# Row-wise exponentials of 16 attention heads on ScalarE: one instruction over a shifted copy, or 16 instructions that read the scores with the row maximum as bias and give the row sum

## What is computed

```python
q = l2norm(q) * qs; k = l2norm(k) * ksc          # then rotary tables
sim = einsum('bhwie,bhwje->bhwij', bq, bk2) * QK_SCALE    # 32 x 64 scores, QK_SCALE = 8
sim = where(mask, -finfo.max, sim)
attn = softmax(sim, -1)                          # row maximum, exp, row sum
out = einsum('bhwij,bhwje->bhwie', attn, bv2)
x = (out @ Wo) + x
x = ffn_layer(shift_tokens(x)) + x
```

## Time and profile before

| | |
|---|---|
| time, median of 2 runs | 4887.01 us (4881.81 and 4892.21) |
| span of the profiled execution | 4869.5 us |
| what lies around the span | 12.3 us and 22.7 us against the two runs |
| busy: PE, DVE, ACT, POOL | 78%, 79%, 51%, 49% of the span |
| granted TensorE clock, mean | 0.905 |
| scalar exponentials of attention (L743) | 192, 1060 ns each |

### The profile page before, as it was taken

One profiled execution on the slowest core, in us unless ns is written; L12 is line 12 of the kernel. 1 busy time (PEld: TensorE's weight loads), 2 busy tenths in 40 slices (PEclk: granted clock), 3 DMA queues, 4 the chain that ended last, 5 costly groups with the idle time before them and its releaser, 6 DMA issues.

```text
span 4869.5 us, 152986 instructions
## 1 busy us (share of the span) xinstructions
PE 3785.1 (78%) x64080; PEld 2581.5 (53%) x64080; DVE 3828.5 (79%) x6082; ACT 2483.4 (51%) x3705; POOL 2389.1 (49%) x1426
## 2 busy tenths in 40 slices
PE   5887887787787787788777877877877887887887
PEld 3554554554555455456435645554554554554554
DVE  4886886896896897797448878877976886986896
ACT  3554554554554565455225545554554554553553
POOL 3663563563664564455006535544553653553552
PEclk9998899899899999888878989999988998998999
DMA  2221221221221222122002212221221221221221
GB/s 82 54 57 46 53 55 48 53 54 44 58 56 51 49 57 58 40 55 63 6 10 51 57 47 51 56 57 43 57 58 39 55 59 40 57 55 44 53 57 46
DMA packets 179337, 247.34 MB, mean 51 GB/s; under 512 B 52516, under 2 KB 75040, under 8 KB 177184
## 3 DMA queue, kind: packets, MB, share of 16 engines
q1 hardware_dynamic: 178976, 242.09, 19.6%
HBM read 39.51 MB, written 1.05 MB: 8 GB/s over the span
## 4 chain that ended last, share of the span: by engine, by line
PE 35%; POOL 18%; DVE 17%; ACT 10%; issue 8%; DVEq 7%; SPq 3%; DMA 1%; ACTq 0%; POOLq 0%
POOL V L1185 9%; PE PS L390 6%; PE PS L544 5%; POOL V L1191 5%; POOL V L1193 5%; PE PS L382 4%; PE PS L466 3%; PE PS L416 3%; DVEq L1000 3%; DVE QN L927 3%; PE PS L383 2%; PE PS L384 2%; DVEq L921 2%; PE PS L576 2%; ACT PR L743 2%
## 5 line engine op out<-in xcount | busy, mean ns | idle before, releaser
L1185 POOL TENSOR_TENSOR V<-QN,TAB 128x512 f32<-128x512 f32 x768 | 1116.7, 1485 | 1791.2 <-DVE QN L927 1791.2
L382 PE MATMUL PS<-WH,XH 128*128 128x512 f32 x1152 | 634.4, 551 | 427.8 <-DVE XL L945 338.8
L697 ACT ACTIVATE RAWQK<-PS 128x1024 f32<-128x1024 f32 x384 | 392.3, 1022 | 848.5 <-PE PS L384 808.1
L934 DVE TENSOR_TENSOR U<-QN,TAB 128x1024 f32<-128x1024 f32 x384 | 736.8, 1922 | 16.4 <-issue 15.3
L390 PE MATMUL PS<-EYE,V 128*128 128x128 f32 x3072 | 449.6, 285 | 188.0 <-POOL V L1193 107.8
L1191 POOL TENSOR_TENSOR V<-V,U 128x1024 f32<-128x1024 f32 x192 | 516.6, 2690 | 81.3 <-DVE U L934 60.8
L382 PEld LDWEIGHTS PS<-WH,XH 128*128 128x128 f32 x1152 | 241.5, 210 | 560.4 <-DVE XL L945 210.3
L1193 POOL TENSOR_TENSOR V<-V,U 128x1024 f32<-128x1024 f32 x192 | 453.6, 2362 | 140.4 <-DVE U L934 140.4
L390 PEld LDWEIGHTS PS<-EYE,V 128*128 128x128 f32 x3072 | 366.1, 147 | 276.6 <-POOL V L1193 139.8
L384 PE MATMUL PS<-WL,XH 128*128 128x512 f32 x1152 | 511.2, 444 | 0.0
L383 PE MATMUL PS<-WH,XL 128*128 128x512 f32 x1152 | 511.0, 444 | 0.0
(11 more groups left out here) (150 smaller groups left out, 6509.1 us busy)
## 6 DMA issues: line engine op xcount, KB each, us to landing
V<-VS SPq DMA_DIRECT2D x3072, 64.0 KB, 2.0
U<-wqkv SPq DMA_DIRECT2D x13, 1024.0 KB, 5.2
V<-wqkv SPq DMA_DIRECT2D x13, 512.0 KB, 6.8
WO<-wo SPq DMA_DIRECT2D x13, 512.0 KB, 3.8
W<-w SPq DMA_DIRECT2D x12, 341.0 KB
ROT<-c_rot SPq DMA_DIRECT2D x1, 2048.0 KB, 10.4
QKS<-qks SPq DMA_DIRECT2D x13, 128.0 KB, 3.7
W<-w SPq DMA_DIRECT2D x12, 114.0 KB
```

Of the source, the lines that this page charges most:

```text
L382: pe.matmul(o, XH[:, p, :], WH[:, w], start=True, stop=False)
L934: dve.tensor_tensor(paired(U[:, k]), split(QN[:, k]), per_dim(TAB[:, 2 * k * DH:(2 * k + 1) * DH], DH), ALU.mult).then_inc((u_q, u_k)[k], 1)
L1185: ins = pool.tensor_tensor(paired(V[:, k])[:, :, :, h * half:(h + 1) * half], split(QN[:, k])[:, :, :, (1 - h) * half:(2 - h) * half], per ...
```

## The change

The subtraction SM and the row sum of VectorE go. VectorE now multiplies the 16 row maxima of a partition by -8 (NB) and signals `nb_ready`. ScalarE computes exp(8 * score + NB) straight from the score banks in PSUM, head by head, since a bias is one value per partition: 16 instructions of 128 x 64 take the place of one of 128 x 1024, and each gives the row sum as a second output into SUM. The last one signals `e_ready`. TensorE's mask, which overwrites the scores, now waits for `e_ready` where it waited for `sm_ready`; so does the first hidden product of the feed-forward part. VectorE's wait for `e_ready` stands before the reciprocal. A separate tile K4S replaces the part of SM that the linear-attention block used.

```diff
-        SM = sb("SM", [P, HEADS, 2 * WIN])
+        NB = sb("NB", [P, HEADS])
+        K4S = sb("K4S", [P, GT])
...
-        K4 = SM[:, :, :].rearrange("p a b -> p (a b)")[:, 0:GT].rearrange("p (j d) -> p j d", d=P)
+        K4 = K4S[:, :].rearrange("p (j d) -> p j d", d=P)
...
                     pe.wait_ge(halo_ready, c(0))
                     if past(i, 2):
-                        pe.wait_ge(sm_ready, c(-1))
+                        pe.wait_ge(e_ready, c(-1))
                     for r in range(2):
                         pe.matmul(PS[:, SB + r, :], EYEB[:, :],
...
-                    pe.wait_ge(sm_ready, val(pe, lay * CH + (inv * DEPTH + 1) * CH))
+                    pe.wait_ge(e_ready, val(pe, lay * CH + (inv * DEPTH + 1) * CH))
...
                 if cc:
-                    act.wait_ge(sm_ready, c(-1))
+                    act.wait_ge(nb_ready, c(-1))
                     if past(i, 3):
                         act.wait_ge(pt_ready, c(-2))
                         act.wait_ge(rs_ready, c(-2))
-                    act.activation(paired(PR[:, :, :]), split(SM[:, :, :]), ACT.Exp,
-                                   scale=QK_SCALE).then_inc(e_ready, 1)
+                    for h in range(HEADS):
+                        r, j = h % 2, h // 2
+                        ins = act.activation(PR[:, h, :], PS[:, SB + r, j * 2 * WIN:(j + 1) * 2 * WIN], ACT.Exp,
+                                             bias=NB[:, r * NP_ + j:r * NP_ + j + 1], scale=QK_SCALE,
+                                             accum_out=SUM[:, h:h + 1])
+                    ins.then_inc(e_ready, 1)
...
                     dve.tensor_reduce(MX[:, :], sc, AX.X, ALU.max)
                     dve.drain()
-                    dve.tensor_tensor(SM[:, :, :], sc, rep(MX[:, :], [P, HEADS, 2 * WIN], 2),
-                                      ALU.subtract).then_inc(sm_ready, 1)
+                    dve.tensor_scalar(NB[:, :], MX[:, :], -QK_SCALE, None, ALU.mult).then_inc(nb_ready, 1)
...
-                if cc:
-                    dve.wait_ge(e_ready, c(-1))
-                    dve.tensor_reduce(SUM[:, :], PR[:, :, :], AX.X, ALU.add)
                 if a or cc:
                     dve.drain()
                 if cc:
+                    dve.wait_ge(e_ready, c(-1))
                     dve.reciprocal(SUM[:, :], SUM[:, :]).then_inc(rs_ready, 1)
```

More of the change, by code:

```diff
@@ L190, in build @@
         tevq = sem("tevq"); tevq1 = sem("tevq1"); tev0 = sem("tev0"); tev1 = sem("tev1"); halo_ready = sem("halo_ready")
-        s_ready = sem("s_ready"); sm_ready = sem("sm_ready"); e_ready = sem("e_ready")
+        s_ready = sem("s_ready"); nb_ready = sem("nb_ready"); e_ready = sem("e_ready")
         rs_ready = sem("rs_ready"); on_ready = sem("on_ready"); to_ready = sem("to_ready")
```

## The result

The changed kernel takes 5672.98 us (5672.36 and 5673.59) against 4887.01 us: 1.161 times as long, interval 1.158 to 1.165. Forecast were 5,870 us in a range of 5,380 to 6,450. A mark such as the earlier trace rows names the group of rows of the kernel before that a view is to be read beside.

The account below looks back on a forecast made before the run. The bound was taken as a loop through XL, TensorE, ON, transposes, ScalarE's queue and XH, nearly equal to VectorE's own. 4869.5 + 756 + 24 + 200 = 5,850 us of span, 5,870 us as time; range 5,380 to 6,450.

Parts of the forecast that it names:

- The ring: Loop per step: XL, TensorE, ON, transposes, ScalarE's queue with the exponential, XH, XL; 19.27 us before, 23.5 after.
- the mask's wait: TensorE's mask must now wait for the exponentials, putting mask and transposes behind them: 1.55 us in 15 of 16 steps.
- the fall of the clock: TensorE idle 5.6 us per step drops to half clock on mask and transposes: 1.1 us in 180 steps, 200 us.
- XL to ON: From XL's end to ON's start, 3.99 us before, 2.95 forecast without VectorE's sum.
- sixteen exponentials, to the mask: ScalarE's sixteen exponentials with their sums at 0.35 us each: 5.6 us, bounds 3.3 to 9.8, where one took 1.05.
- mask and transposes, with the clock: TensorE's mask and second-half transposes behind the exponentials: 1.55 us at full clock, plus 1.1 for half clock.
- second evacuation to the end of XL: ScalarE's second evacuation through XH to VectorE's XL, chain as before: 5.92 us plus 0.03 for its release, 5.95.
- Rival B: TensorE runs at half speed from mask to next output projection: 450 us clock loss instead of 200, 6,120 us; chance 17%.
- The subtraction: VectorE's subtraction ahead of QN goes; its 1.2 us per step are worth nothing, as VectorE is early there.
- Rival D: VectorE sets the pace, so removing its subtraction and sum gives 411 us: 4,476 us; chance 2%.
- The sum on VectorE behind XL: Without it ON starts about 0.1 us after TensorE's products with v, gaining 1.04 us per step.
- Rival C: The sixteen exponentials stream, 0.85 us in all: 4,790 us, not slower; deciding point 0.08 us each; chance 3%.

Follow-up runs that it names:

- the run with TensorE kept busy: Changed kernel plus 22 bf16 products that nobody reads, ahead of TensorE's wait for the mask; 5437.8 us, 1.114 of the kernel before.
- the run of VectorE's part alone: Changed kernel with one exponential straight from the score banks, no maximum in it, VectorE summing 4 of 64 keys; 5002.6 us, 1.023 of the kernel before.
- the exchange of order: Changed kernel with the transposes of the second half of q and k ahead of the mask in TensorE's program; 5273.5 us, 1.079 of the kernel before.
- half the instructions: Changed kernel with eight exponentials of 128 x 128 for sixteen of 128 x 64, head pairs sharing bias and sum; 5249.5 us, 1.074 of the kernel before.

## Why the prediction was right

The ring was the right one, and so were the order of its parts, the mask's wait and the fall of the clock. The sizes were not all right: 5,870 - 4,887 = 983 us were forecast and 786 came, a quarter too much. The terms of the ring, forecast and measured in the rows above:

| step | forecast, us | measured, us |
|---|---|---|
| XL to ON | 2.95 | 326.61 - 323.63 = 2.98 |
| ON to the end of the transposes | 6.42 | 6.49 (309.35 - 302.86) |
| to the exponentials | 1.00 | 310.35 - 309.35 = 1.00 |
| sixteen exponentials, to the mask | 5.6 | 315.33 - 310.35 = 4.98 |
| mask and transposes, with the clock | 1.55 + 1.1 | 318.09 - 315.33 = 2.76 |
| second evacuation to the end of XL | 5.95 | 323.63 - 318.09 = 5.54 |
| sum | 24.6 | 23.75 |

(The transposes' end, 309.35, is 1.04 us behind their start at 308.31.)

- *The price of the exponentials* was the largest mis-sized term: 5.6 for 4.98 us, of which 4.7 are the sixteen and the rest is the last one's end. 0.35 each was taken from bounds of 0.205 and 0.615. The lower bound is what they cost without the read (0.21), and the read adds 0.08: ScalarE overlaps the two, where I took the overlap away. The Trainium skill ("ScalarE: Activation LUTs", What ACT_TABLE_LOAD costs) gave 3.8 us without the read; the run without the read measured 3.4. These 3.8 us are an estimate from the page's figures; with the measured read it would be 5.1, where the train with its reads took 4.7.
- *The end of the ring* came out 0.4 us shorter, and two errors against each other are in that: the closeness is partly luck. From the second evacuation to the end of XH are 321.89 - 318.09 = 3.80 us where they were 3.44 (238.17 - 234.73), since the transposes of the exponentials were slow too (1.44 us for 1.06). The two halves of XL took 1.57 us (322.06 to 323.63), of which the second half 0.29 where it took 1.25, and GpSimd's products had ended at 323.18, just ahead of it. In the kernel before they ran beside both halves:

```profile
237.96 5.08 POOL L1185 TENSOR_TENSOR V<-QN,TAB 128x512 f32<-128x512 f32 x4 [5.08 <-DVE QN L927]
```

- *The clock* cost 1.21 us on mask and transposes (2.76 - 1.55), near the 1.1 forecast, and some 0.4 on the transposes of the exponentials, which the forecast had at nothing. In the run with TensorE kept busy both come back, 1.6 us in the step shown. The time fell by 1.3 us per step; XL's halves took 0.27 us longer there on average (431 + 1138 ns for 710 + 592). Rival B, twice the forecast, did not come: the projections behind XL ran at full clock.
- *The subtraction* was worth nothing in the changed kernel, as said: 7.07 us of waiting ahead of XL in the step shown. Rival D falls with the run of VectorE's part alone.
- *The sum on VectorE behind XL*: ON started 0.1 us after the products with v, as forecast. But the forecast gave all of the 1.04 us to the missing sum. The run without the second output has the sum back and loses 0.2 us of them, since the rotation between XL and ON takes 1.16 us there, as in the changed kernel, and not 1.97 as before. By these rows either of the two alone nearly gives the gain.
- *Rival C* falls by the spacing of 0.29 us; its threshold was 0.08.
- *The signs*: the wait ahead of the mask (5.29 us), the step (23.56) and the clock (0.855) are as forecast. The spacing of 0.29 us lies just below 0.3 to 0.4, ScalarE's 3,212 us below 3,300, VectorE's wait of 7.07 us above the 5, and its busy time of 3,142 us well below 3,400; the last section has the reason for that one.

Against the kernel before, the ring's terms change so in the steps shown: exponentials +3.93 us (4.98 for 1.05), mask and transposes +2.76 (they lay beside the exponential), XL to ON -1.01, ON to the exponentials +0.07, second evacuation to XL -0.38. That is +5.4, and the step grew by 4.3 on average, since the ring before sums to 18.4 us by the same terms (3.99 + 6.42 + 1.00 + 1.05 + 5.92) and its steps took 19.27 on average: the ring was not the only thing that set its pace. The largest single term is the exponentials. Four runs price parts of the loss in the time: the exchange of order 400 us, the clock 235, the read 289 with VectorE's sum put back, half the instructions 423. They overlap and aren't a sum.

## What to carry to other kernels

Before moving work from the busiest engine, follow one step of the pipeline round: here an engine at 79% with a second loop as long beside it gave back 89 us of 411, and the engine at 51% held the ring. When a consumer reads a PSUM bank in place of a copy, the next writer of that bank waits for it; put everything that doesn't need the bank ahead of that write. And look at what TensorE does next after a new wait: here it paid 1.6 us per step at half clock behind the wait itself.

## What the runs showed of the hardware

- A second output of an activation is an instruction of its own, ACTIVATION_READ_ACCUMULATOR, 261 ns on average in its row but 0.08 us in the time. Spacing of 128 x 64 exponentials: 0.15 us from SBUF without bias, 0.24 with the read; 0.21 from PSUM with bias, 0.29 with the read. Source and bias were not varied apart.
- In the train from PSUM the durations grow from 0.32 to 0.42 us while the starts stay 0.29 apart; in the one from SBUF with the read they stay at 0.24. 16 x the mean duration (367 ns) would be 5.9 us; the train took 4.7. Trains are to be priced from start to start.
- VectorE's rotation fell from 1922 to 1274 ns on average, and GpSimd's products from 1485 to 1314, in the same code: in the changed kernel they stand less beside each other. VectorE's busy time fell by 686 us; the subtraction and the sum less the new product NB are 385 of them (235 + 234 - 85), the rotation 249 and the halves of XL 68, while other groups rose a little. XL's first half shows it within the kernel before: 1.05 us at 238.34, with GpSimd's products at work since 237.96, and 0.28 us at 257.62, with the products starting at 257.84. That the overlap is the cause is inferred from the timelines; no run varied it alone. The Trainium skill ("GPSIMD Engine Reference", Specifications) says that the SBUF interfaces of GpSimd are shared with VectorE, with contention when a VectorE instruction has two inputs in SBUF; the rotation has two (QN and TAB), as XL has (XA and XH), and the rows agree.
